# A three-block language-model tower: the FP4 quantiser as two list steps, four groups of VectorE work on GpSimd, new step lists

## The reference, cut to what matters

```python
emb = w0[inputs] @ w1 * mask * 16                      # 512 -> 256
h = layer_norm(x); hx = token_shift(h)
k, v, r = (h*m + hx*(1-m)) @ wk, wv, sigmoid(... @ wr)
# the recurrence: out = (e1*aa + e2*v) / (e1*bb + e2), carried on stably along time
x = x + (r * wkv) @ wo
kk = relu(mix_k(layer_norm(x)) @ cwk) ** 2             # 256 -> 1024
x = x + sigmoid(mix_r @ cwr) * (kk @ cwv)

def fp4_quant_dequant(x):                              # blocks of 16 along the last dim
    scale = max(abs(xb)) / 6
    return GRID[searchsorted(MID, abs(xb / scale))] * sign(xb) * scale
g, u = fp4_linear(norm(x), w_gate), fp4_linear(norm(x), w_up)     # 256 -> 704
x = x + fp4_linear(silu(g) * u, w_down)                # 704 -> 256
```

## Time and profile before

| | |
|---|---|
| time, median of 3 runs | 774.72 us (774.24 to 775.47) |
| span of the profiled execution | 772.5 us |
| TensorE busy | 701.0 us (91%) |
| VectorE busy | 591.7 us (77%) |
| ScalarE busy | 509.2 us (66%) |
| GpSimd busy | 144.3 us (19%) |

### The profile page before, as it was taken

The page is one execution under the profiler, slowest core; times in us unless marked ns, Lnnn a source line. Parts: engine busy times, 40 slices in busy tenths (PEclk is TensorE's granted clock), DMA queues, the critical chain, the costliest instruction groups (busy, mean ns, idle before and its releaser), DMA issues.

```text
span 772.5 us, 9862 instructions
## 1 busy us (share of the span) xinstructions
PE 701.0 (91%) x3301; PEld 563.6 (73%) x3301; DVE 591.7 (77%) x1023; ACT 509.2 (66%) x888; POOL 144.3 (19%) x220
## 2 busy tenths in 40 slices
PE   4465788899999999999999999999999999899676
PEld 3325656787788867886788777896888777788574
DVE  0678777888788879788778878887988878872763
ACT  2556796698568966597749866797749774861221
POOL 2403301430032302230142103230232003000000
PEclk9687899999999999999999999999999999899999
DMA  4800000000010000010010001000010000000000
GB/s 124 275 2 27 3 25 2 27 10 20 15 41 1 28 14 14 28 28 1 14 42 2 28 15 41 1 28 10 4 42 1 1 14 15 1 0 14 15 0 28
DMA packets 13374, 19.34 MB, mean 25 GB/s; under 512 B 982, under 2 KB 10764, under 8 KB 13324
## 3 DMA queue, kind: packets, MB, share of 16 engines
q1 hardware_dynamic: 10720, 10.31, 4.1%
q0 software_dynamic: 2560, 8.39, 3.7%
q10 hardware_dynamic: 44, 0.01, 0.0%
HBM read 14.51 MB, written 4.19 MB: 24 GB/s over the span
## 4 chain that ended last, share of the span: by engine, by line
PE 74%; DVE 11%; ACT 9%; issue 4%; DMA 1%; POOL 0%; ACTq 0%; DVEq 0%; POOLq 0%
PE psB L556 20%; PE psC L652 11%; PE psC L625 11%; PE psB L583 11%; PE psA L547 9%; PE psA L519 5%; PE psC L639 3%; PE psA L507 2%; ACT hT L745 1%; ACT mix L754 1%; DMA rows<-L_tok_w,ids_now 1%; DVE top L360 1%; ACT take L800 1%; PE psA L529 1%; PE psC L611 1%
## 5 line engine op out<-in xcount | busy, mean ns | idle before, releaser
L556 PE MATMUL psB<-cwv_s,kkT 128*128 128x256 f32 x512 | 113.9, 380 | 0.0
L556 PEld LDWEIGHTS psB<-cwv_s,kkT 128*128 128x128 f32 x512 | 96.2, 190 | 15.7 <-issue 3.3
L652 PE MATMUL psC<-downT,hqT 128*128 128x256 f32 (+1 forms) x384 | 96.7, 397 | 0.0
L625 PE MATMUL psC<-up_hi,xq_hi 128*128 128x352 f32 x256 | 88.2, 345 | 9.2 <-DVE xq_lo L1202 8.5
L547 PE MATMUL psA<-mix,kvr_s 128*128 128x512 f32 x192 | 88.6, 606 | 3.4 <-ACT vT L776 2.4
L652 PEld LDWEIGHTS psC<-downT,hqT 128*128 128x128 f32 (+1 forms) x384 | 69.4, 192 | 26.4 <-issue 19.0
L625 PE MATMUL psC<-up_hi,xq_lo 128*128 128x352 f32 x256 | 83.8, 327 | 0.0
L625 PE MATMUL psC<-up_lo,xq_hi 128*128 128x352 f32 x256 | 83.6, 327 | 0.0
L447 POOL TENSOR_SCALAR sc_c<-mv_c 128x2 f32<-128x2 f32 x16 | 7.0, 436 | 371.7 <-DVE mv_c L1134 371.7
L547 PEld LDWEIGHTS psA<-mix,kvr_s 128*128 128x128 f32 x192 | 36.5, 194 | 42.4 <-issue 39.3
L519 PE MATMUL psA<-w_s,rowsT 128*128 128x256 f32 x256 | 59.5, 386 | 0.0
(11 more groups left out here) (163 smaller groups left out, 1488.5 us busy)
## 6 DMA issues: line engine op xcount, KB each, us to landing
out<-h SPq DMA_DIRECT2D x16, 256.0 KB, 2.1
mix<-L_attn_cwk SPq DMA_DIRECT2D x1, 1024.0 KB, 8.0
...
rows<-L_tok_w,ids_now POOLq DMA_INDIRECT x32, 4.0
```

The lines of the kernel that those rows point to most:

```text
L556: mm = nc.tensor.matmul(psB[:, B.slot(name), q * D:(q + 1) * D], lhsT[:, k, (2 * j + q) * P:(2 * j + q + 1) * P], weight[:, k, :], start=( ...
L625: mm = nc.tensor.matmul(psC[:, C.slot(name), f, 0:INTER // 2], a[:, k, t * P:(t + 1) * P], b[:, w, k, f * (INTER // 2):(f + 1) * (INTER // ...
L652: mm = nc.tensor.matmul(psC[:, C.slot(name), 0, q * D:(q + 1) * D], hqT[0:n, q, k, :], downT[0:n, k, :], start=(k == 0), stop=(k == KI - 1))
```

## The change

The quantiser of activations is cut at the square into two steps of VectorE's list: `c_sn`, `c_sq` (four operations, scaling) and `c_rn`, `c_rq` (three, rounding). So other steps can stand between them. The buffer `square` becomes two, used in turn. `newv`, `numer`, `b_low` and the second half of `b_value` (now `b_final0`, `b_final1`) go to GpSimd, with a semaphore `wkv_sums` for the first two. The tile y goes into the memory of takev, so takev's first columns are cleared again for each chunk and `a_y` waits for `wkv_sums`; the scales and statistics get memory of their own. All lists are new. The lines that matter:

```diff
-WKV = ["pad"] + [f"{step}{d}" for step in ("top", "gain", "now", "takev", "sumv", "sum1", "newv", "numer", "denom",
-                                           "near", "fix", "avg", "att")
-                 for d in range(H)]
+WKV = ["pad", "padv"] + [f"{step}{d}" for step in ("top", "gain", "now", "takev", "sumv", "sum1", "denom", "near", "fix",
+                                                   "avg", "att")
+                         for d in range(H)]
+
+WKV_SUMS = [f"{step}{d}" for step in ("newv", "numer") for d in range(H)]
...
+SCALED, ROUNDED = 4, 3
...
+            def newv_a(ch):
+                for d in range(H):
+                    at(pool, wkv_exp, ch, EXPS.index(f"new{d}") + 1)
+                    A.wait_emptied(pool, ch, f"v{d}")
+                    A.wait_full(pool, ch, "v1")
+                    nc.gpsimd.tensor_tensor(numer[:, d], e_new[:, d], vT[:, d], ALU.mult).then_inc(wkv_sums.sem, 1)
+
+            def numer_a(ch):
+                for d in range(H):
+                    at(pool, wkv, ch, WKV.index(f"sumv{d}") + 1)
+                    at(pool, wkv_sums, ch, WKV_SUMS.index(f"newv{d}") + 1)
+                    nc.gpsimd.tensor_tensor(numer[:, d], numer[:, d], takev[:, d, :, 0:T], ALU.add).then_inc(wkv_sums.sem, 1)
+
+            def low_b(ch):
+                for d in range(H):
+                    at(pool, b_high, ch, d + 1)
+                    if d == 0:
+                        B.wait_full(pool, ch.back(1), "kk7")
+                    nc.gpsimd.tensor_tensor(key_lo[:, d], mix2[:, 0, d].rearrange("p c t -> p (c t)"), key_hi[:, d].bitcast(F32),
+                                            ALU.subtract).then_inc(b_low.sem, 1)
+
+            def final_b(j):
+                def step(ch):
+                    at(pool, b_sum, ch, 1)
+                    B.wait_emptied(pool, ch, f"cv{j}")
+                    pair = slice(2 * j, 2 * j + 2)
+                    nc.gpsimd.tensor_tensor(h1[:, ch.parity, pair, :], h1[:, ch.parity, pair, :], rr[:, pair, :], ALU.add
+                                            ).then_inc(b_fin.sem, 1)
+                return step
...
             def y_a(ch):
                 at(act, a_coef, ch, 7)
-                B.wait_emptied(act, ch.back(1), "o1")
+                at(act, wkv_sums, ch, len(WKV_SUMS))
...
-                    at(act, quant, ch, QUANT * (t + 2) + 4)
-                    nc.scalar.activation(square[:], hq[:, t], ACT.Square, scale=SPREAD).then_inc(squared.sem, 1)
+                    at(act, scaled, ch, SCALED * (t + 3))
+                    at(act, rounded, ch, ROUNDED * (t + 1))
+                    nc.scalar.activation(square[:, t % 2], hq[:, t], ACT.Square, scale=SPREAD).then_inc(squared.sem, 1)
...
                 def f_near(d):
                     expd(f"inv{d}")
+                    at(dve, wkv_sums, ch, WKV_SUMS.index(f"newv{d}") + 1)
                     return tt(e_new[:, d], keep[:, d, :, now], take[:, d, :, now], ALU.mult)
...
                 def f_fix(d):
                     after(f"near{d}")
+                    at(dve, wkv_sums, ch, WKV_SUMS.index(f"numer{d}") + 1)
...
+                return t.unsqueeze(2).to_broadcast([P, nb, BLOCK])
+
+            def scale_blocks(ch, n, data, nb):
+
+                big, scale = scales[:, n % 2, 0, 0:nb], scales[:, n % 2, 1, 0:nb]
+                done = SCALED * n
+                at(dve, rounded, ch if n >= 2 else ch.back(1), ROUNDED * ((n - 2) % (2 + TILES) + 1))
+                nc.vector.tensor_reduce(big, blocks(data), AX_X, ALU.max, apply_absolute_value=True).then_inc(scaled.sem, 1)
+                at(dve, scaled, ch, done + 1)
+                nc.vector.tensor_scalar(scale, big, 1.0 / 6.0, 1e-12, ALU.mult, ALU.max).then_inc(scaled.sem, 1)
+                at(dve, scaled, ch, done + 2)
+                nc.vector.reciprocal(big, scale).then_inc(scaled.sem, 1)
+                at(dve, scaled, ch, done + 3)
+                nc.vector.scalar_tensor_tensor(out=blocks(data), in0=blocks(data), scalar=NUDGE, in1=wide(big, nb),
+                                               op0=ALU.mult, op1=ALU.mult).then_inc(scaled.sem, 1)
+
+            def round_blocks(ch, n, data, nb):
+
+                w, scale = square[:, n % 2, 0:nb * BLOCK].bitcast(F32), scales[:, n % 2, 1, 0:nb]
+                done = ROUNDED * n
+                at(dve, squared, ch, n + 1)
+                at(dve, scaled, ch, SCALED * (n + 1))
+                nc.vector.scalar_tensor_tensor(out=data, in0=w, scalar=MAGIC, in1=data, op0=ALU.add, op1=ALU.add
+                                               ).then_inc(rounded.sem, 1)
+                at(dve, rounded, ch, done + 1)
+                nc.vector.scalar_tensor_tensor(out=data, in0=w, scalar=MAGIC, in1=data, op0=ALU.add, op1=ALU.subtract
+                                               ).then_inc(rounded.sem, 1)
+                at(dve, rounded, ch, done + 2)
+                nc.vector.scalar_tensor_tensor(out=blocks(data), in0=blocks(data), scalar=-1.0, in1=wide(scale, nb),
+                                               op0=ALU.mult, op1=ALU.mult).then_inc(rounded.sem, 1)
```

More of the change, by code:

```diff
@@ L66 @@
 ORDER = {
[5 rows of a table removed]
-    "act": [("c_cols1", 1), ("w_par", -3), ("b_cols", 0), ("b_part", 0), ("c_up1", 1), ("a_emb1", -1),
[7 rows of a table removed]
-    "dve": [("c_split1", 4), ("b_mix", 3), ("a_stat", 2), ("c_up1", 4), ("w_par", -3), ("b_low", 3), ("w_quant2", 3),
[5 rows of a table removed]
-        ("b_coef", -2)],
-    "sp": [("c_down1", 2), ("c_down0", 1)],
[20 rows of a table added]
+    "pool": [("a_coef", -2), ("a_newv", -2), ("a_numer", -2), ("b_final0", -1), ("c_coef0", -1), ("b_final1", -1),
+        ("gather1", -3), ("c_coef1", -1), ("b_sum", -2), ("b_coef", -2), ("gather0", -4), ("b_low", -2)],
+    "sp": [("c_down0", -1), ("c_down1", -1)],
 }
@@ L485, in coef_c @@
                 return step
-            walk("pool", {"gather0": gather(0), "gather1": gather(1), "a_coef": coef_a, "b_sum": sum_b, "b_coef": coef_b, "c_coef0": coef_c(0), "c_coef1": coef_c(1)})
+            walk("pool", {"gather0": gather(0), "gather1": gather(1), "a_coef": coef_a, "a_newv": newv_a, "a_numer": numer_a, "b_sum": sum_b, "b_low": low_b, "b_final0": final_b(0), "b_final1": final_b(1), "b_coef": coef_b, "c_coef0": coef_c(0), "c_coef1": coef_c(1)})
         @block.tensor
@@ L766, in project @@
             def project(name):
-                dst, last = {"k": (kT, "gain"), "v": (vT, "newv"), "r": (rT, None)}[name]
+                dst, last = {"k": (kT, "gain"), "v": (vT, "takev"), "r": (rT, None)}[name]
                 def step(ch):
@@ L1043, in wkv_a, with f_denom @@
                 both(2, lambda d: nc.vector.tensor_tensor_scan(long(take, d), long(keep, d), long(take, d), 0.0, ALU.mult, ALU.add))
-                def f_newv(d):
+                def f_denom(d):
                     expd(f"new{d}")
-                    A.wait_full(dve, ch, "v1")
-                    return tt(numer[:, d], e_new[:, d], vT[:, d], ALU.mult)
-                both(2, f_newv)
-                def f_numer(d):
-                    after(f"newv{d}")
-                    return tt(numer[:, d], numer[:, d], takev[:, d, :, before], ALU.add)
-                both(3, f_numer)
-                def f_denom(d):
                     after(f"sum1{d}")
@@ L1098, in mix_b @@
                 shifted_mix(ch, hT2, mix2, MIX_B, b_part, b_mixed)
-            def low_b(ch):
-                for d in range(H):
-                    at(dve, b_high, ch, d + 1)
-                    if d == 0:
-                        B.wait_full(dve, ch.back(1), "kk7")
-                    nc.vector.tensor_tensor(key_lo[:, d], mix2[:, 0, d].rearrange("p c t -> p (c t)"), key_hi[:, d].bitcast(F32),
-                                            ALU.subtract).then_inc(b_low.sem, 1)
             def key_w(_):
@@ L1141, in step, with pair_c, scale_c @@
+            def pair_c(j):
+                return normc[:, 2 * j:2 * j + 2].rearrange("p t d -> p (t d)")
+            def scale_c(j):
                 def step(ch):
                     at(dve, c_norm, ch, 2 * (j + 1))
-                    at(dve, quant, ch if j else ch.back(1), QUANT if j else QUANT * (2 + TILES))
-                    quantise(dve, [part(0, normc[:, 2 * j:2 * j + 2].rearrange("p t d -> p (t d)"), square[:, 0:2 * D], P,
-                                        2 * D // BLOCK)], quant.sem, lambda k: quant.count(ch, QUANT * j + k),
-                             (squared.sem, lambda k: squared.count(ch, j + k)))
+                    scale_blocks(ch, j, pair_c(j), 2 * D // BLOCK)
+                return step
@@ L1147, in quant_c, with round_c, step @@
+            def round_c(j):
+                def step(ch):
+                    round_blocks(ch, j, pair_c(j), 2 * D // BLOCK)
                 return step
```

50 lines of the change are left out of this document (27 added, 23 removed), and 37 rows, old and new, of the table ORDER.

## The result

The changed kernel takes 780.20 us (median of 4 runs, 778.42 to 782.02), the kernel before 774.55 in the same session: ratio 1.007, 95% interval 1.0052 to 1.0088. It is slower by 0.7%, 5.6 us. The forecast was 767.8, with a range of 761 to 779.

The account below looks back on a forecast made before the run. TensorE, busy 504.21 of 506.95 us in the steady periods, was taken as the bound, so gains must come from the ends. Filling -0.9, steady 0, draining -6.0 sum to -6.9 us from 774.72: 767.8 us, range 761 to 779.

Parts of the forecast that it names:

- What the two engines cost each other: VectorE's scans beside GpSimd's moved work: delay of 2.4 us per recurrence, bounds 0 and 4.7; +4.7 us for the filling's two.
- The rival with its 4.7 us: Full exclusion of VectorE and GpSimd: each recurrence pays 4.7 us, total 778.5 us; chance 0.22.
- The filling: Pipeline fill before the steady periods: -5.6 us from moved work and orders, +4.7 from engine hindrance, together -0.9 us.
- the change around `w_sq1`: Filling, ScalarE: `w_sq1` goes behind `b_norm`, VectorE's weight rounding ahead of `b_mix`; +1.0 us, bounds -1.5 and +2.1.
- The term of `w_turn2`: Filling, TensorE: turn of w_down done ahead of the value products instead of before `c_cols0`; -2.4 us, at least 1.6.
- The steady period: Six periods of 84.5 us: TensorE's steps the same, delay of 2.4 us hidden in a slack of 3.7; sum 0.
- third rival: Second chain over GpSimd late: TensorE waits 0.5 to 1 us a period in `c_up0` or `c_cols1`; 771 to 774 us; chance 0.15.
- second rival: Full exclusion: 4.7 us per recurrence exceeds the tile 3 copies' slack, so TensorE waits in `c_down1`; 778.5 us; chance 0.22.
- The draining: Pipeline drain at the end: split quantiser and new order shorten it by 6.0 us, at least 3.5, at most 8.
- The four tiles: Draining, VectorE's quantiser work on four tiles: 28.7 us in the new order instead of 33.1, so -4.4 us.
- the two shorter waits for xq_lo: Last turn but one: two waits of the same kind as the draining's 4.91 us, 1.9 us, of which 1.1 taken.
- The exclusion rival: GpSimd and VectorE fully exclude each other: filling +3.8, periods +6.0, draining -6.0, sum +3.8, 778.5 us; chance 0.22.

## Why the prediction was wrong

**What the two engines cost each other.** This is the step that failed. The forecast took half of 4.7 us for each recurrence, 2.4, on the ground that small GpSimd operations had left VectorE's pairs at 1.21 us. The measured delay is 8.5 - 4.5 = 4.0 us. Unchanged VectorE steps beside operations of a few columns said nothing of operations of 128x512. The rule of the Trainium skill (page "SBUF — State Buffer", section "Who interferes with whom"), which the forecast weighed and put at half, was right here: 4.5 us of scans and 5.1 of GpSimd work took 9.0 together. The row to trust was the 0.78 us against 0.23, the only one in which an engine had been held up. The rival with its 4.7 us was nearer; `newv` starts 0.5 us ahead of the scans in chunk 0 and 0.2 in chunk 1, and the four scans take 8.5 us in both.

**The filling** was forecast at -0.9 and is +4.8. It can be cut at points that both traces have. Times are us. The last column has the forecast's terms, each in the stretch where it lies, rounded:

| stretch | before | now | difference | forecast |
|---|---|---|---|---|
| start to the first scan of chunk 0 | 50.49 | 52.72 | +2.2 | 0 |
| first scan to the end of `att`, chunk 0 | 15.88 | 17.27 | +1.4 | 0 |
| to chunk 1's `a_emb0` | 5.02 | 5.20 | +0.2 | 0 |
| to the first scan of chunk 1 | 49.64 | 50.60 | +1.0 | +1.0 |
| first scan to the end of `att`, chunk 1 | 15.71 | 17.70 | +2.0 | +0.6 |
| to chunk 2's `a_emb0` | 8.74 | 6.77 | -2.0 | -2.4 |

Each column is of one profile, and a stretch with TensorE's work in it can differ by 1.5 us between profiles (chunk 1's `a_emb0` starts at 75.19 here and at 76.70 with `c_down1` early, where nothing ahead of it was changed). The recurrences are steadier. They are 2.8 us over their forecast. The delay of 4.0 in the place of 2.4 gives 2 x 1.6 = 3.2, and the run with `newv` and `numer` on VectorE takes 3.1 us less in them. The 2.2 us at the start are `w_turn0`, which the forecast left out: moved back, it gives them back, though the end of the filling then gains only 0.3. The +1.0 of the fourth stretch is right by luck. It was taken for the change around `w_sq1`; but with `b_final` alone on GpSimd that stretch is 48.83 us, 0.8 shorter than before. What fills it up in the changed kernel is, as far as the runs show, `b_low` (1.7 to 2.2 us), costed at nothing behind TensorE's gate product: in the filling that cover isn't there. The term of `w_turn2`, -2.4, was right by itself.

**The steady period** was forecast at 0 and lost 0.8 us a period. The sum looked for the slack of the recurrence in the copies ahead of `c_down1`, found 3.7 us, and there was indeed no wait there. The delay of 4.0 us went another way: `c_down1`'s sum late, store late, `b_sum` late, and so beside a small operation of `c_sn1`. This is the third rival's place (`c_cols1`) and size (0.5 to 1 us a period) with the second rival's cause; they had been priced as if independent. Its link on the DMA queue was in neither.

**The draining** was forecast at -6.0 and gave -3.2. In the run with `b_final` alone on GpSimd it is 765.8 - 646.88 = 118.92 us against 124.97 before, -6.05. But that agreement is in part luck. The four tiles, forecast at -4.4, give -3.5 in that run. Its last `c_down1` runs at the upper level of the clock in 5.93 us, where the kernel before needed 7.62 at a mean of 0.78: 1.7 us that no term of the forecast had. The profile with everything on VectorE, where the same products took 8.08 us, drains in 122.0 us, 3.0 less than before. Only the term of the tiles is the same in these profiles: product to last rounding is 29.7 us in the changed kernel too (736.84 to 766.53), against 33.1 before. It falls short of its -4.4 because of one wait. `c_down0`'s sum was to lie in tile 3's wait at no cost; it waits 2.12 us itself there, where the waits for the square of tiles 1 and 2 are 0.86, since TensorE reaches `c_down0` only behind tile 3's up product.

```profile
757.65 0.88 DVE L1213 TENSOR_TENSOR hq<-psC,hq 128x704 f32<-128x704 f32 x1
...
763.19 0.69 DVE L1231 TENSOR_TENSOR h<-h,psC 128x512 f32<-128x512 f32 x1 [2.12 <-PE psC L688]
763.79 0.88 DVE L1185 SCALAR_TENSOR_TENSOR hq<-square,hq 128x704 f32<-128x704 f32 x1
```

The wait of 4.91 us for xq_lo went as predicted: it is 0.87 now. The 1.1 us from the two shorter waits for xq_lo did not come: from the first cut of the draining to tile 0's product it is 80.7 us, against 79.4 before.

The range of 761 to 779 missed the time by 1.2 us at its slow end. The exclusion rival, 778.5, had +3.8, +6.0 and -6.0 for the three parts; measured are +4.8, +3.9 and -3.2. It is near in the sum by errors that offset each other, and its wait in the middle of `c_down1` doesn't exist.

**A faster version.** With newv, numer and b_low on VectorE, and b_final on either engine, the changed kernel takes 768.5 us: 0.8% below the kernel before and 1.5% below the change.
